# Layer 0 of a two-layer attention and mixture-of-experts kernel: other PSUM banks and other units for the small products

## The chip, the cores and the metric

The kernel runs on one core of a Trainium2 chip. The metric is the time of one execution on the device in microseconds. Each engine (TensorE, VectorE, ScalarE, GpSimd and the queue engine SyncE) runs its own list of instructions in order, and the engines hold each other by semaphores.

## What is computed

The input `x` has 64 batches of 64 channels by 256 positions, and `ctx_2048` has the same shape. Two layers follow each other, and each has an attention part and a mixture-of-experts part:

```python
x = x + _L0_xattn_ref(_layernorm(x), ctx_2048, ...)   # 8 heads of 8 channels, rotary, softmax over 256 positions
x = x + _L0_ffn_ref(_layernorm(x), ...)               # 64 experts, the best 8 of each row, silu(g) * u
x = x + _L1_xattn_ref(_layernorm(x), ctx_2048, ...)   # the same attention without rotary and output projection
x = x + _L1_ffn_ref(_layernorm(x), ...)               # 64 experts with a capacity
# _L0_xattn_ref, per batch:
q, k, v = heads(Wq x + bq), heads(Wk c + bk), heads(Wv c + bv)
q, k = rotary(q), rotary(k)
out = softmax(q k^T / sqrt(8)) v
return Wo out + bo
```

## The kernel before

The 64 batches are handled as 32 pairs; a pair fills the 128 partitions (2 batches of 64 channels). The attention stage of a layer is a software pipeline of 41 steps. A pair passes through it in stages that lie a fixed number of steps apart (`LAG`): load, comb, front (projection and rotation of q and k), stack (rearranging them by DMA), smax (row maxima of the scores), attn (exponentials and value products), back (division, output projection, residual), route (router logits), place and post (choice of slots, scatter). So one step works on up to eight pairs at once, each in another stage: pair s-2 is in front, s-4 in smax, s-5 in attn, s-6 in back, s-7 in route.

Each step has 16 units. In every unit TensorE makes one score product (`scores`, bank `psS`) for the pair in smax and the transposed score products (`scores_t`, two matmuls, bank `psE`) for the pair in attn; VectorE takes the maximum of the first (`red`), and ScalarE the exponential of the second (`prob`). Value products follow in groups of sixteen after units 7, 11, 15 and 2 of the next step. All else is placed by hand at fixed units: the instructions of an engine in a unit are issued in the order in which the `if` lines stand.

The small products share two PSUM banks, `psM[0]` and `psM[1]`. `MISC` lists them in the order in which TensorE makes them in a step, each with its stage; in the kernel before an item's bank is its place in the list modulo 2. `Step.before(item)` finds the item that used the same bank last, and `bank()` makes TensorE wait until that one has been read (`FREE`: for `OT0` and `OT1` the writing of `nrm`, for `V` the copy to `v`, for `K` and `Q` the rotation, for `NT` the write of `nt`, for `XT` the copy `xT`, for `mT0` the write of `mlo`). In layer 0 the banks are in this order: `mT1` 0, `RK` 1, `V` 0, `K` 1, `OT0` 0, `OT1` 1, `Q` 0, `NT` 1, `mT0` 0, `XT` 1, `WO` 0, `LG` 1.

The items that the change touches:

- `Q` (`q_rows`, line 1567, made by `product`, line 1564): two float32 products of the layer-normalised rows `xn`, for q and for q with its channels rolled. `xn` is made by ScalarE (line 963), which needs `rstd` from GpSimd (`roots`, lines 785 to 790). VectorE rotates the result (`rotate(0)`, lines 1157 and 1159), and GpSimd sums the halves (`rotated`, line 798).
- `OT0`, `OT1` (line 1562): the attention output `osb`, transposed, two transposes for each group of heads h. Each row holds 8 sums per head and the sum of exponentials. VectorE inverts that (`invert`, line 1139) and multiplies (`normalise`, line 1147) into `nrm`.
- `NT` (line 1562): `nrm` transposed back, two transposes; ScalarE writes it with its bias to `nt` (line 946), which `WO` (unit 12) multiplies by the output projection.
- `mT0` (line 1562): the maxima of the first half of the units, transposed; ScalarE makes their high part `mhi` (line 910), VectorE the low part `mlo` (line 1132), and SyncE sends both to the stacked `q` (line 686). The transposed scores of unit 0 of the next step wait for them.
- `XT` (line 1562, unit 10): `xr` transposed for the router; ScalarE copies it to `xT` (line 955).

Of the kernel before, what the change touches and what calls it, by code (L numbers as in the profile page):

```python
# [31 lines left out]
P = 128  # L32
B, C, T = 64, 64, 256
NH, HC = 8, 8
PAIRS = B // 2
TOKENS = B * C
E, I, K = 64, 96, 8
# [3 lines left out]
HALF = 16  # L41
# [68 lines left out]
def units_of_sum(s0):  # L110
    if s0 >= FULL:
        return ADDED, TWO, ONE, ALL, MOMENTS
    if s0 == FULL - 1:
# [9 lines left out]

MISC = {
    layer: [("mT1", "attn"), ("RK", "place"), ("V", "smax"), ("K", "front"), ("OT0", "back"), ("OT1", "back"),
            ("Q", "front"), ("NT", "back"), ("mT0", "smax"), ("XT", "route"), *last]
    for layer, last in enumerate(((("WO", "back"), ("LG", "route")), (("LG", "route"), ("LIST", "post"))))
}


class Step:
# [40 lines left out]
    def before(self, item):  # L172

        names = [name for name, _ in MISC[self.L]]
        i = names.index(item)
        bank, s = i % 2, self.s0
        while s >= 0:
            i -= 2
            if i < 0:
                i, s = i + len(names), s - 1  # L180
            if (self.L, s, names[i]) == (1, FULL - 2, "Q"):
                continue
            if 0 <= s - LAG[MISC[self.L][i][1]] < PAIRS and s >= 0:
                return bank, MISC[self.L][i], Step(self.L, s, self.it)
        return bank, None, None

# [11 lines left out]
def build(nc, x, ctx, tables, wts, out):  # L198
    stack = ExitStack()
    with stack:  # L200
# [231 lines left out]
        def lastbuf(st, stage, per=16):  # L432
# [3 lines left out]

        FREE = dict(mT0=s_mlo[0], mT1=s_mlo[1], V=s_v, OT0=s_nrm[0], OT1=s_nrm[1], Q=s_qr, K=s_kr,
                    NT=s_nt, WO=s_x1, XT=s_xT, LG=s_logit, RK=s_tot, LIST=s_list)
# [21 lines left out]

        def head_cols(tile, o, n):

            return tile[:, 0:2 * P].rearrange("p (h r) -> p h r", r=HALF)[:, :, o:o + n]

# [5 lines left out]
        def item_bank(L, name):  # L470
            return [n for n, _ in MISC[L]].index(name) % 2

# [414 lines left out]
        def _(act):  # L887
# [5 lines left out]
            def body(st):  # L893
# [19 lines left out]
                for u in range(UNITS):  # L913
# [27 lines left out]
                    if u == 3:  # L941
                        o_out("back", 1)
                    if L == 0 and u == 8 and st.on("back"):
                        act.wait_ge(s_ntp, st.n("back"))
                        wait(act, s_wo, last(st, "back"))
                        a.activation(nt[:, :], psM[item_bank(0, "NT")][:, 0:T], ACT.Identity,
                                     bias=bias[:, 7:8]).then_inc(s_nt, 1)
# [4 lines left out]
                    if u == (10, 11)[L] and st.on("route"):  # L952
                        act.wait_ge(s_xtp, st.n("route"))
                        wait(act, s_lgp, last(st, "route"))
                        a.copy(xT[:, :, :].rearrange("p c t -> p (c t)"), psM[item_bank(L, "XT")][:, 0:2 * P]).then_inc(s_xT, 1)
                    if u == 9 and st.on("smax"):
                        max_rows("smax", 0)
                    if u == (14 if filled else 6) and (st.on("front") or st.on("route")):
                        act.wait_ge(s_rstd, 4 * st.roots())
                    if u == (14 if filled else 6) and st.on("front"):  # L960
                        b = st.buf("front")
                        wait(act, s_qp, last(st, "front", back=NB))
                        a.activation(xn[b][:, :], (xin, x2)[L][b][:, :], ACT.Identity, bias=rstd[:, 1, 0:1],
                                     scale=rstd[:, 0, 0:1]).then_inc(s_xn, 1)
# [75 lines left out]
        def _(dve):  # L1040
# [77 lines left out]
            def body(st):  # L1118
# [16 lines left out]
                def invert(h):  # L1135

                    ps = psM[item_bank(L, f"OT{h}")]
                    dve.wait_ge(s_ot[h], st.n("back"))
                    ch.add(v_.reciprocal(rec[:, h, :], head_cols(ps, 8, 1).rearrange("p h o -> p (h o)")), f"rec{h}")

                def normalise(h):

                    ps = psM[item_bank(L, f"OT{h}")]
                    wait(dve, s_ntp, last(st, "back"))
                    ch.join(f"rec{h}")
                    r = rec[:, h, :]
                    v_.tensor_tensor(nrm[:, h, :].rearrange("p (h c) -> p h c", c=HC), head_cols(ps, 0, HC),  # L1147
                                     bass.AP(r.tensor, r.offset, [list(r.ap[0]), [1, UNITS], [0, HC]]),
                                     ALU.mult).then_inc(s_nrm[h], 1)

                def rotate(i):

                    b = st.buf("front")
                    ps = psM[item_bank(0, "QK"[i])]
                    dve.wait_ge((s_qp, s_kp)[i], st.n("front"))
                    wait(dve, s_qk, last(st, "front"))
                    v_.scalar_tensor_tensor(rope[:, 0, i, :], ps[:, 0:T], bias_c[:, 2 * i:2 * i + 1], cos[:, :],
                                            ALU.add, ALU.mult)
                    v_.scalar_tensor_tensor(rope[:, 1, i, :], ps[:, T:2 * T], bias_c[:, 2 * i + 1:2 * i + 2], sin[:, :],
                                            ALU.add, ALU.mult).then_inc((s_qr, s_kr)[i], 1)  # L1160
# [49 lines left out]
                for u in range(UNITS):  # L1210
# [21 lines left out]
                    if L == 1 and u == 8 and st.on("back"):  # L1232
# [5 lines left out]
                                                xres[b][:, :], ALU.add, ALU.add).then_inc(s_x1, 1)  # L1238
                    if u == 10 and st.on("smax") and not filled:
                        split_max("smax", 0)  # L1240
# [37 lines left out]
                    if L == 0 and u == 4 and st.on("front"):  # L1278
                        if st.s0 == LAG["front"]:
                            dve.wait_ge(d_table, 16 * 3 * HC)  # L1280
                        rotate(1)
                    if u == 5 and st.on("back"):
                        invert(0)
                    if u == 6 and st.on("back"):
                        normalise(0)
                        invert(1)
                    if u == 7 and st.on("back"):
                        normalise(1)
                    if L == 0 and u == 7 and st.on("front"):
                        rotate(0)  # L1290
                    if u == 0 and st.on("post") and L == 1:
# [213 lines left out]
        def _(pe):  # L1505
# [3 lines left out]
            def body(st):  # L1509
# [62 lines left out]
                for u in range(UNITS):  # L1572
# [11 lines left out]
                    if u == 2:  # L1584
                        values("back", 3)
                    if u == 7 and st.on("front") and not (L == 1 and st.s0 == FULL - 2):
                        q_rows(st)
# [6 lines left out]
                    if u == 3 and st.on("smax"):  # L1594
                        b = st.buf("smax")
                        product("V", "smax", [(d_ctx[b], st.nbuf("smax"))],
                                [(ctx_t[b][:, i * P:(i + 1) * P], wbd[L]["v"][:, :]) for i in range(2)], s_vp, P)
                    if u in (5, 6) and st.on("back"):
                        h = u - 5
                        product(f"OT{h}", "back", [(s_oev, st.n("back", 2))],  # L1600
                                [(osb[:, half, h * P:(h + 1) * P], None) for half in range(HALVES)], s_ot[h])
                    if u == 8 and st.on("back"):
                        product("NT", "back", [(s_nrm[0], st.n("back")), (s_nrm[1], st.n("back"))],
                                [(nrm[:, h, :], None) for h in range(2)], s_ntp)
                    if u == 9 and st.on("smax"):
                        product("mT0", "smax", [(s_max, st.n("smax", UNITS, 8))],
                                [(mx[st.buf("smax")][:, 0, :], None)], s_mT[0])
# [142 lines left out]
```

## Time and profile before

| | us |
|---|---|
| median of 3 runs | 2037.71 (2036.14 to 2038.18) |
| the profiled execution | 2035.62 |
| its span | 2033.8 |
| TensorE matmuls busy | 1634.2 (80%) |
| VectorE busy | 1412.9 (69%) |
| ScalarE busy | 1230.3 (60%) |
| GpSimd busy | 986.1 (48%) |

The shares are means over the attention stage of layer 0 (to about 600 us), its expert stage, the attention stage of layer 1 and its expert stage, which have different limits. For the change the reader needs the first stage alone, and in it one step of the pipeline.

### The profile page before, as it was taken

To read this page: it belongs to the slowest core of one execution; us is meant where nothing else is said; L and a number is where in the kernel's file an instruction comes from. 1 tells how busy PE (TensorE), PEld (TensorE's weight loads), DVE (VectorE), ACT (ScalarE), POOL (GpSimd) and SP (SyncE) were. 2 spreads that over 40 slices of the span, in tenths; PEclk is the share of its full clock that TensorE was granted. 3 is DMA by queue.
4 is the path that set the end of the run, shared out by engine and by line. 5 is a ranking of instruction groups with operands and counts; after the bars stand their busy time and mean duration, and the time that the engine had idled before them with its cause. 6 is when DMAs were issued, how large, how long until landed. Compare 5 with 4: busy or idle time off the path is not lost. (4 is left out here: it accounts for less than half of the span.)

```text
span 2033.8 us, 44372 instructions
## 1 busy us (share of the span) xinstructions
PE 1634.2 (80%) x12470; PEld 1095.2 (54%) x12623; DVE 1412.9 (69%) x4341; ACT 1230.3 (60%) x3174; POOL 986.1 (48%) x1114
## 2 busy tenths in 40 slices
PE   3999999999974999999997278888888888855551
PEld 1555555555543889888886134444444444444430
DVE  5888899999954445545434489999999999743330
ACT  1777777777752566666665268778878777621110
POOL 4367777777763000000001776666666662158883
PEclk9999999999986999999999589999999999979996
DMA  5688878777757976666665678887877775178856
GB/s 141 159 211 249 240 215 217 214 216 213 207 159 225 289 213 202 195 200 198 196 199 169 163 188 219 224 224 198 202 193 195 197 198 144 49 198 185 176 93 112
DMA packets 413085, 390.94 MB, mean 192 GB/s; under 512 B 46640, under 2 KB 385072, under 8 KB 412848
## 3 DMA queue, kind: packets, MB, share of 16 engines
q1 hardware_dynamic: 346496, 265.28, 49.2%
q0 software_dynamic: 37904, 90.22, 16.9%
q10 hardware_dynamic: 28448, 32.59, 5.5%
q8 instruction: 111, 1.82, 0.4%
q14 instruction: 126, 1.03, 0.2%
HBM read 233.74 MB, written 170.16 MB: 199 GB/s over the span
## 5 line engine op out<-in xcount | busy, mean ns | idle before, releaser
L1125 DVE TENSOR_REDUCE mx<-psS 128x2 f32<-128x512 f32 x1024 | 679.0, 674 | 86.5 <-PE psS L1518 59.0
L923 ACT ACTIVATE prob<-psE 128x512 f32<-128x512 f32 x1024 | 594.4, 591 | 235.8 <-PE psE L1531 219.2
L772 POOL DMA_INDIRECT yg<-y_d,row_all x256 | 248.4, 970 | 630.8 <-SPq L413 480.0
L1531 PE MATMUL psE<-q,k 128*128 128x256 bf16 x2048 | 394.1, 275 | 30.7 <-issue 10.2
L1518 PE MATMUL psS<-k,q 128*128 128x512 bf16 x871 | 336.5, 388 | 27.0 <-DVE mx L1125 14.1
L1470 DVE TENSOR_TENSOR hid<-sil,psE 128x96 f32<-128x96 f32 x384 | 97.7, 254 | 331.0 <-ACT sil L1024 331.0
L1643 PE MATMUL psE<-wt,xgT 128*128 (+1 forms) x1536 | 323.9, 335 | 2.1 <-ACT xgT L1019 1.6
L759 POOL DMA_INDIRECT xs_d<-xr,row_all x256 | 251.5, 982 | 94.4 <-ACT prob L923 46.1
L1531 PEld LDWEIGHTS psE<-q,k 128*128 128x128 bf16 x2048 | 187.1, 98 | 181.3 <-ACT prob L923 62.6
L1549 PE MATMUL psO<-prob,v 128*32 128x256 f32 x4096 | 275.0, 386 | 0.0
L1019 ACT COPY xgT<-psS 128x256 f32<-128x256 f32 x384 | 144.6, 376 | 186.7 <-PE psS L1637 160.7
L1643 PEld LDWEIGHTS psE<-wt,xgT 128*128 128x128 f32 x1536 | 246.6, 194 | 7.8 <-issue 5.9
L1637 PE MATMUL psS<-ident,xg 128*128 128x128 f32 x768 | 153.9, 282 | 104.7 <-DMA xg<-xn_d,idx 88.8
L1655 PE MATMUL psM<-wt,hT 96*128 (+1 forms) x768 | 231.5, 383 | 0.0
L1637 PEld LDWEIGHTS psS<-ident,xg 128*128 128x128 f32 x768 | 103.5, 143 | 165.4 <-DMA xg<-xn_d,idx 92.0
L1518 PEld LDWEIGHTS psS<-k,q 128*128 128x128 bf16 x1024 | 103.6, 101 | 146.8 <-issue 87.4
L1028 ACT COPY y_all<-psM 128x256 f32<-128x256 f32 x320 | 119.1, 372 | 87.9 <-PE psM L1655 87.6
L1549 PEld LDWEIGHTS psO<-prob,v 128*32 128x32 f32 x4096 | 107.1, 109 | 95.7 <-issue 47.7
L1024 ACT ACTIVATE sil<-psE 128x96 f32<-128x96 f32 x384 | 96.3, 251 | 93.1 <-PE psE L1643 92.4
L1655 PEld LDWEIGHTS psM<-wt,hT 96*128 96x128 f32 x768 | 117.0, 193 | 14.8 <-issue 0.4
L1564 PE MATMUL psM<-xn,proj_q 128*128 128x256 f32 x126 | 44.5, 436 | 86.8 <-DVE nrm L1147 50.4
L818 POOL TENSOR_TENSOR parts<-rem,parts 128x512 bf16<-128x512 f32 x64 | 74.7, 1168 | 44.2 <-ACT parts L997 42.6
(220 smaller groups left out, 2539.0 us busy)
## 6 DMA issues: line engine op xcount, KB each, us to landing
xg<-xs_d SPq DMA_DIRECT2D x320, 128.0 KB, 2.6
y_d<-y_all SPq DMA_DIRECT2D x320, 128.0 KB, 2.3
q<-q_stack_d SPq DMA_DIRECT2D x128, 256.0 KB
k<-k_stack_d SPq DMA_DIRECT2D x128, 256.0 KB
wt<-in_gu ACTq DMA_DIRECT2D x110, 192.0 KB, 2.9
q_stack_d<-parts SPq DMA_DIRECT2D x64, 192.0 KB
k_stack_d<-parts SPq DMA_DIRECT2D x64, 192.0 KB
wt<-in_dn ACTq DMA_DIRECT2D x110, 96.0 KB, 3.6
```

The costliest lines, as they stand in the source:

```text
L759: g.indirect_dma_start(xs_d[:, :], bass.IndirectOffsetOnAxis(row_all[:, row(st.pair(stage) * K + k, 1)], 0), xr[b][:, 0:T], None).then_inc ...
L772: g.indirect_dma_start(yg[:, k, :], None, y0_d[:, :], bass.IndirectOffsetOnAxis(row_all[:, row(st.pair("load") * K + k, 1)], 0))\
L923: a.activation(prob[gr][:, u % 4, :], psE[ring][:, :], ACT.Exp, scale=SCALE).then_inc(s_exp, 1)
L1019: a.copy(xgT[st.buf("X", 2)][:, :, :].rearrange("p c t -> p (c t)"), psS[st.buf("X", 2)][:, 0:2 * P]).then_inc(s_xgT, 1)
L1028: a.copy(y[st.buf("D")], psM[st.buf("D", 2)][:, 0:T]).then_inc(s_y, 1)
L1125: v_.tensor_reduce(mx[b][:, bg // 4, :].rearrange("p (h r) -> p h r", h=2)[:, :, (bg % 4) * 2 + tt], psS[(UNITS * (st.s0 - LAG["smax"]) + ...
L1518: m_.matmul(psS[(UNITS * (st.s0 - LAG["smax"]) + u) % 3][:, :], q2[b][:, bg, tt * P:(tt + 1) * P], k2[b][:, bg, :], start=True, stop=True) ...
L1531: ins = m_.matmul(psE[ring][:, i * T:(i + 1) * T], k2[b][:, bg, hh * T + i * P:hh * T + (i + 1) * P], q2[b][:, bg, :], start=True, stop=True)
L1549: ins = m_.matmul(psO[32 * j:32 * j + 32, half * T:(half + 1) * T], v[b][:, i, unit_at(4 * q + j), :], prob[gr][:, j, i * T:(i + 1) * T], ...
L1637: ins = m_.transpose(psS[i][:, c * P:(c + 1) * P], xg[b][:, c * P:(c + 1) * P], ident[:, :])
L1643: ins = m_.matmul(psE[i][:, 0:2 * I], xgT[i][:, c, :], weights_of(st, "GU", table, P, 2 * I * c, 2 * I), start=(c == 0), stop=(c == 1))
L1655: m_.matmul(psM[i][:, 0:T], hT[i][:, :], weights_of(st, "D", table, I, 4 * I, T), start=True, stop=True).then_inc(s_yp, 1)
```

## The change

In layer 0 alone `MISC` now names the bank of each item, and the order is another: `mT1` 0, `RK` 1, `V` 0, `K` 1, `Q` 0, `OT` 1, `NT` 0, `mT0` 1, `XT` 0, `WO` 0, `LG` 1. `OT0` and `OT1` become one item `OT` of four transposes, all in bank 1. The units become:

| | before | after |
|---|---|---|
| `xn` on ScalarE, with the wait for `rstd` | 6 | 4, ahead of the copy of `v` |
| `Q` on TensorE | 7 | 5 |
| rotation of q on VectorE | 7 | 6 |
| transposes of the output | 5 and 6 | 6 |
| `invert` and `normalise` | 5, 6, 7 | all at 7 |
| `NT` on TensorE, `nt` on ScalarE | 8 | 9 |
| `mT0`, `mhi` | 9 | 10 |
| `mlo` of the first half | 10 | 11 |

Layer 1 keeps its banks and units. The core of the diff:

```diff
-MISC = {
-    layer: [("mT1", "attn"), ("RK", "place"), ("V", "smax"), ("K", "front"), ("OT0", "back"), ("OT1", "back"),
-            ("Q", "front"), ("NT", "back"), ("mT0", "smax"), ("XT", "route"), *last]
-    for layer, last in enumerate(((("WO", "back"), ("LG", "route")), (("LG", "route"), ("LIST", "post"))))
-}
+MISC = (
+    (("mT1", "attn", 0), ("RK", "place", 1), ("V", "smax", 0), ("K", "front", 1), ("Q", "front", 0),
+     ("OT", "back", 1), ("NT", "back", 0), ("mT0", "smax", 1), ("XT", "route", 0), ("WO", "back", 0),
+     ("LG", "route", 1)),
+    (("mT1", "attn", 0), ("RK", "place", 1), ("V", "smax", 0), ("K", "front", 1), ("OT0", "back", 0),
+     ("OT1", "back", 1), ("Q", "front", 0), ("NT", "back", 1), ("mT0", "smax", 0), ("XT", "route", 1),
+     ("LG", "route", 0), ("LIST", "post", 1)),
+)
...
-                    if L == 0 and u == 8 and st.on("back"):
+                    if L == 0 and u == 9 and st.on("back"):
...
-                    if u == 9 and st.on("smax"):
+                    if u == (10, 9)[L] and st.on("smax"):
                         max_rows("smax", 0)
-                    if u == (14 if filled else 6) and (st.on("front") or st.on("route")):
+                    if u == (14 if filled else (4, 6)[L]) and (st.on("front") or st.on("route")):
                         act.wait_ge(s_rstd, 4 * st.roots())
-                    if u == (14 if filled else 6) and st.on("front"):
+                    if u == (14 if filled else (4, 6)[L]) and st.on("front"):
...
-                    if u == 10 and st.on("smax") and not filled:
+                    if u == (11, 10)[L] and st.on("smax") and not filled:
                         split_max("smax", 0)
...
-                    if u == 5 and st.on("back"):
+                    if L == 0 and u == 6 and st.on("front"):
+                        rotate(0)
+                    if u == (7, 5)[L] and st.on("back"):
                         invert(0)
-                    if u == 6 and st.on("back"):
+                    if u == (7, 6)[L] and st.on("back"):
+                        if L == 0:
+                            invert(1)
                         normalise(0)
-                        invert(1)
+                        if L == 1:
+                            invert(1)
                     if u == 7 and st.on("back"):
                         normalise(1)
-                    if L == 0 and u == 7 and st.on("front"):
-                        rotate(0)
...
-                    if u == 7 and st.on("front") and not (L == 1 and st.s0 == FULL - 2):
+                    if u == (5, 7)[L] and st.on("front") and not (L == 1 and st.s0 == FULL - 2):
                         q_rows(st)
...
-                    if u in (5, 6) and st.on("back"):
+                    if L == 0 and u == 6 and st.on("back"):
+                        pe.wait_ge(s_oev, st.n("back", 2))
+                        ps = bank(pe, st, "OT")
+                        for h in range(2):
+                            for half in range(HALVES):
+                                ins = m_.transpose(ps[:, (2 * h + half) * P:(2 * h + half + 1) * P],
+                                                   osb[:, half, h * P:(h + 1) * P], ident[:, :])
+                            ins.then_inc(s_ot[h], 1)
+                    if L == 1 and u in (5, 6) and st.on("back"):
...
-                    if u == 8 and st.on("back"):
+                    if u == (9, 8)[L] and st.on("back"):
                         product("NT", "back", [(s_nrm[0], st.n("back")), (s_nrm[1], st.n("back"))],
                                 [(nrm[:, h, :], None) for h in range(2)], s_ntp)
-                    if u == 9 and st.on("smax"):
+                    if u == (10, 9)[L] and st.on("smax"):
                         product("mT0", "smax", [(s_max, st.n("smax", UNITS, 8))],
```

In layer 0 `invert` of either half waits for both pairs of transposes (`s_ot[1]`), and the readers of the banks follow the new layout.

## Rows read from the trace of the kernel before

**Rows 1.** Busy time by stretch: one step of the pipeline.

```profile
core 0: us, PE busy (x) PEld busy (x) DVE busy (x) ACT busy (x) POOL busy (x), PEclk, DMA share, GB/s
...
299.83:317.00 17.17, 16.12 (x141) 9.58 (x142) 15.52 (x47) 12.62 (x29) 12.82 (x16) 1.00 0.72 208
```

**Rows 2.** Waits from 100 to 650 us: total, times, longest.

```profile
ACT prob L923 <- PE psE L1531: 118.7, 152, 2.2
...
PE psM L1564 <- DVE nrm L1147: 20.5, 26, 0.8
```

**Rows 3.** TensorE in order of time, units 4 to 7: start, length, instruction.

```profile
312.71 0.66 PE L1564 MATMUL psM<-ctx,proj_k 128*128 128x256 f32 x2
...
313.64 0.38 PE L1518 MATMUL psS<-k,q 128*128 128x512 bf16 x1
313.85 0.38 PE L1531 MATMUL psE<-q,k 128*128 128x256 bf16 x2
314.07 0.38 PE L1562 MATMUL psM<-ident,osb 128*128 128x128 f32 x2
...
314.86 0.41 PE L1562 MATMUL psM<-ident,osb 128*128 128x128 f32 x2
315.32 0.38 PE L1531 MATMUL psE<-q,k 128*128 128x256 bf16 x2
316.49 0.67 PE L1564 MATMUL psM<-xn,proj_q 128*128 128x256 f32 x2 [0.79 <-DVE nrm L1147]
...
317.52 0.85 PE L1549 MATMUL psO<-prob,v 128*32 128x256 f32 x12
```

**Rows 4.** TensorE in order of time, units 7 to 10 and the next unit 0.

```profile
300.35 1.07 PE L1549 MATMUL psO<-prob,v 128*32 128x256 f32 x16
301.36 0.39 PE L1518 MATMUL psS<-k,q 128*128 128x512 bf16 x1
...
301.80 0.38 PE L1562 MATMUL psM<-ident,nrm 128*128 128x128 f32 x2
...
303.11 0.41 PE L1562 MATMUL psM<-ident,xr 128*128 128x128 f32 x2
...
308.78 0.38 PE L1531 MATMUL psE<-q,k 128*128 128x256 bf16 x2 [0.16 <-issue]
```

**Rows 5.** ScalarE in order of time, units 8, 4, 5 and 6.

```profile
302.00 0.60 ACT L923 ACTIVATE prob<-psE 128x512 f32<-128x512 f32 x1 [2.19 <-PE psE L1531]
302.50 0.47 ACT L946 ACTIVATE nt<-psM,bias 128x256 f32<-128x256 f32 x1
...
312.91 0.60 ACT L923 ACTIVATE prob<-psE 128x512 f32<-128x512 f32 x1 [0.17 <-PE psE L1531]
313.41 0.37 ACT L981 COPY v<-psM 128x256 f32<-128x256 f32 x1
314.27 1.25 ACT L923 ACTIVATE prob<-psE 128x512 f32<-128x512 f32 x2 [0.50 <-PE psE L1531]
315.42 0.59 ACT L963 ACTIVATE xn<-xin,rstd 128x256 f32<-128x256 f32 x1
```

**Rows 6.** VectorE in order of time, units 4 to 6.

```profile
313.84 0.48 DVE L1157 SCALAR_TENSOR_TENSOR rope<-psM,bias_c,cos 128x256 f32<-128x256 f32 x1 [0.26 <-PE psM L1564]
...
314.63 0.68 DVE L1125 TENSOR_REDUCE mx<-psS 128x2 f32<-128x512 f32 x1
...
315.30 0.25 DVE L1139 RECIPROCAL rec<-psM 128x16 f32<-128x16 f32 x1
315.47 0.63 DVE L1125 TENSOR_REDUCE mx<-psS 128x2 f32<-128x512 f32 x1
...
316.07 0.27 DVE L1147 TENSOR_TENSOR nrm<-psM,rec 128x128 f32<-128x128 f32 x1
```

**Rows 7.** GpSimd in order of time: the last of the root operations.

```profile
311.58 0.19 POOL L790 TENSOR_TENSOR rstd<-below,rstd 128x2 f32<-128x2 f32 x1
```

**Rows 8.** SyncE's queue in order of time: the low part of the maxima.

```profile
304.40 0.56 SPq L686 DMA_DIRECT2D q<-mlo  x1
```

More of the change, by code:

```diff
@@ L172, in before @@
     def before(self, item):
-        names = [name for name, _ in MISC[self.L]]
-        i = names.index(item)
-        bank, s = i % 2, self.s0
+        at = [bank for name, _, bank in MISC[self.L] if name == item][0]
+        shared = [(name, stage) for name, stage, bank in MISC[self.L] if bank == at]
+        i, s = [name for name, _ in shared].index(item), self.s0
         while s >= 0:
-            i -= 2
+            i -= 1
             if i < 0:
-                i, s = i + len(names), s - 1
-            if (self.L, s, names[i]) == (1, FULL - 2, "Q"):
+                i, s = i + len(shared), s - 1
+            name, stage = shared[i]
+            if (self.L, s, name) == (1, FULL - 2, "Q"):
                 continue
-            if 0 <= s - LAG[MISC[self.L][i][1]] < PAIRS and s >= 0:
-                return bank, MISC[self.L][i], Step(self.L, s, self.it)
-        return bank, None, None
+            if s >= 0 and 0 <= s - LAG[stage] < PAIRS:
+                return at, (name, stage), Step(self.L, s, self.it)
+        return at, None, None
 def steps(layer, body):
@@ L434, in lastbuf @@
             return st.nbuf(stage, per) - per
-        FREE = dict(mT0=s_mlo[0], mT1=s_mlo[1], V=s_v, OT0=s_nrm[0], OT1=s_nrm[1], Q=s_qr, K=s_kr,
+        FREE = dict(mT0=s_mlo[0], mT1=s_mlo[1], V=s_v, OT=s_nrm[1], OT0=s_nrm[0], OT1=s_nrm[1], Q=s_qr, K=s_kr,
                     NT=s_nt, WO=s_x1, XT=s_xT, LG=s_logit, RK=s_tot, LIST=s_list)
@@ L459, in over_e, with head_cols @@
             return tile.unsqueeze(2).broadcast_to((P, K, n))
-        def head_cols(tile, o, n):
-            return tile[:, 0:2 * P].rearrange("p (h r) -> p h r", r=HALF)[:, :, o:o + n]
+        def head_cols(L, h, o, n):
+            tile = psM[item_bank(L, ("OT", f"OT{h}")[L])]
+            first = (h, 0)[L] * 2 * P
+            return tile[:, first:first + 2 * P].rearrange("p (h r) -> p h r", r=HALF)[:, :, o:o + n]
         def ones_of(b, o):
@@ L470, in item_bank @@
         def item_bank(L, name):
-            return [n for n, _ in MISC[L]].index(name) % 2
+            return [at for n, _, at in MISC[L] if n == name][0]
         FLAG = dict(idx=0, gather=4, X=8, GU=9, H=10, D=11)
@@ L1135, in invert @@
                 def invert(h):
-                    ps = psM[item_bank(L, f"OT{h}")]
-                    dve.wait_ge(s_ot[h], st.n("back"))
-                    ch.add(v_.reciprocal(rec[:, h, :], head_cols(ps, 8, 1).rearrange("p h o -> p (h o)")), f"rec{h}")
+                    dve.wait_ge(s_ot[1 if L == 0 else h], st.n("back"))
+                    ch.add(v_.reciprocal(rec[:, h, :], head_cols(L, h, 8, 1).rearrange("p h o -> p (h o)")), f"rec{h}")
                 def normalise(h):
-                    ps = psM[item_bank(L, f"OT{h}")]
                     wait(dve, s_ntp, last(st, "back"))
@@ L1146, in normalise @@
                     r = rec[:, h, :]
-                    v_.tensor_tensor(nrm[:, h, :].rearrange("p (h c) -> p h c", c=HC), head_cols(ps, 0, HC),
+                    v_.tensor_tensor(nrm[:, h, :].rearrange("p (h c) -> p h c", c=HC), head_cols(L, h, 0, HC),
                                      bass.AP(r.tensor, r.offset, [list(r.ap[0]), [1, UNITS], [0, HC]]),
```

## The prediction, made before the result was known

> **What bounds the kernel now.** I read four views, in this order. First the busy times by stretch [rows 1]: the attention stage of layer 0, to which the whole edit belongs, is a pipeline of 41 steps, and one full step lasts 17.17 us. Its row has TensorE busy for 16.12 us of that at granted clock 1.00, VectorE for 15.52, ScalarE for 12.62, GpSimd for 12.82. So TensorE is the first limit, VectorE is only 1.65 us per step behind it, and the other two have over 4 us to spare. Second the waits of this stage [rows 2]: ScalarE waits 118.7 us for TensorE's transposed scores, which again puts TensorE ahead. TensorE's own waits are few, and the largest is 20.5 us, 26 times 0.79 us, for the normalised rows. Third TensorE's step in order of time [rows 3, 4], with the same stretch of ScalarE and VectorE beside it [rows 5, 6]. The same starts come back 17.17 us later in most steps (some early ones, in which ScalarE also issues weight loads, take 17.63), so I may put 301.36 and 318.53 for the same event.
>
> In rows 3 the reader is to see one hole. The pair of score products of unit 7 ends its slot at 315.54 (315.32 plus 0.22), and the query product behind it begins at 316.49: 0.95 us, of which the profile prints 0.79, as it counts the modelled tail of the matmul as busy. The cause is a bank: the query product writes bank 0, where the item before it is the first transposed result, and that is free only when VectorE has written `nrm` at 316.07, 0.27 long [rows 6]. From 316.34 to 316.49 gives 0.15 us as the time that a release takes to TensorE. The activation of `xn` at 315.42, 0.59 long [rows 5], would have let it go at about 316.16.
>
> **The change part by part.** It happens in the 28 steps in which both a front and a back pair are on (28 of the 41; elsewhere one of the two is missing). Matmul and vector work are the same in amount. What moves is order and three waits. I work the step through again from unit 4, with slots taken from starts: a pair of score products 0.43 (313.64 to 314.07), two transposes 0.22, a projection product of two 0.93 to 1.03 (312.71 to 313.64, 316.49 to 317.52), a group of sixteen value products 1.01 (300.35 to 301.36) [rows 3, 4].
>
> *ScalarE, unit 4.* `xn` now stands between the exponential and the copy of `v`. The exponential begins at 312.91 and gives way after 0.50; `xn` 313.41, the copy at 313.91, its 0.37 us end at 314.28. The exponential of unit 5 can't begin before its scores (314.27 now), so it loses nothing. The moved wait for `rstd` has the `v` copy and all later exponentials behind it; GpSimd's last root operation ends at 311.77 [rows 7], 1.6 us before, so I cost it at nothing; without that cover each late microsecond would be a microsecond of the step.
>
> *TensorE, unit 5.* The query product stands behind the pair that ends at 314.07. It waits for `xn` (314.00) and for bank 0, whose former item is now the value product, so for the copy of `v`: 314.28 plus 0.15 is 314.43. The hole shrinks from 0.95 to 0.36. From both sides: 0.08 if only `xn` held it, 0.6 if the copy came 0.25 later. I take 0.36, because each of its three durations has a row.
>
> *Unit 6 and 7.* The product takes 0.93 to 1.03, I take 0.95: 315.38. Pair to 315.81, four transposes to 316.24, pair to 316.67, value products from 316.75 (the same 0.08 as before) to 317.76. The four transposes need the key product's bank, free since the rotation ended near 314.71. The same bank now makes the second pair of transposes begin at 314.86 and not at 314.72, so 0.14 us goes with it.
>
> *VectorE.* The reduction of unit 6 begins 0.42 after its scores (313.85 to 314.27 is what ScalarE shows for that delay) at 315.80, 0.60 later the rotation of q, 0.79 for its two instructions (313.84 to 314.63), to 317.19; the reduction of unit 7 to 317.79; then two reciprocals at 0.17 (315.30 to 315.47) and two multiplications at about 0.19: the last begins near 318.32 and ends near 318.6. The queue behind these is the reductions of units 8 and 9; they start 0.4 us earlier than in the old step (318.5 against 318.95), so TensorE, which needs them three units later, doesn't wait.
>
> *Unit 9 and 10.* TensorE: pair of unit 8 to 318.20, of unit 9 to 318.64, transposes back at 318.75, held 0.1 by `nrm`. Then the pair of unit 10 and the transposed maxima, and it is at the transposes of `xr` at about 319.5. These use the bank of the transposes back, so they wait for ScalarE's `nt`. ScalarE: exponential of unit 8 at 318.40, of unit 9 at 318.90, `nt` at 319.40, 0.47 long, to 319.87 [rows 5]; plus 0.15 is 320.02. **This is the new hole, 0.5 us.** In the old step there was one unit more between the two, `nt` ended at 302.97 and the transposes of `xr` began at 303.11, hardly held: 0.11. The bounds of the new hole are 0, if something else lets `nt` go earlier, and 0.6.
>
> *Sum.* In the old step the transposes of `xr` begin at 303.11 + 17.17 = 320.28; now at 320.02. Gain 0.26 us a step: 0.59 at the query product and 0.14 at the second transposes, less 0.1 at `nrm`, 0.39 at `nt`, and rounding. What follows in the step is unchanged and moves with it. 28 times 0.26 is 7.3 us. In the four filling and the draining steps one hole shrinks (query product) and the other opens, together 0 within 2 us. Nothing after the stage depends on where in the steps the work stood, and the last steps are paced by exponentials that come earlier as well.
>
> The median is 2037.71 and the profiled execution took 2035.62 with a span of 2033.8, so I expect 2030.4 as a median and about 2026.5 as the span.
>
> *A rule against it.* TensorE's row 314.86 shows two result banks in use in turn, and the change puts four transposes in one. The Trainium skill (Perfetto Trace Analysis, Optimizing Tensor Performance) says that independent groups should rotate through banks, so that the evacuation of one runs beside the next. By that rule the divisions, which now start only after all four transposes, ought to come late and hold TensorE. That they end near 318.6, just where TensorE asks for them, is the row-by-row answer above; what it would cost if the rule wins is rival C.
>
> **The rivals.**
>
> A, *the full hole closes and no new one opens*: `nt` doesn't hold the transposes of `xr`. Then the gain is 0.26 + 0.5, and 28 times 0.76 is 21.3 us: 2016.4. For it: ScalarE is idle 2.19 us just before the exponential of unit 8 [rows 5], so it has room. Against it: the two exponentials and `nt` in a row have 1.47 us of their own from 318.40 on, and TensorE has less than that before it.
>
> B, *the gain is given back at the step's start*. The low part of the first half's maxima moves from unit 10 to 11: VectorE ends it at about 321.7, and the queue issues its transfer at about 321.75 instead of 321.57 (304.40 + 17.17) [rows 8], while the first transposed scores that need it stand 0.26 earlier than 308.78. Now there are 4.38 us between issue and use, then 3.94. No wait for it appears before, so landing takes less than 4.38 as a rule; if it takes more than 3.94 it costs up to 0.44 us a step, 12 us in all, and cancels the gain. With half of that, 2036. The small transfer argues for early landing; the DMA share of 0.72 in this step [rows 1] against.
>
> C, *slower: the divisions bind*. The transposes back may come at 319.0 without moving `nt`, which ScalarE can't begin before 319.40. If VectorE, with only 1.65 us of free time in a step and now with the rotation and a reduction ahead of four small instructions, ends the second multiplication later than about 318.85, every further tenth is on the path. No row shows two reciprocals and two multiplications in a run. If they took their full lengths (0.25 and 0.27 [rows 6]) and were held 0.15 each by the semaphore between them, the end would be near 319.2 and `nt` 0.37 later; with the reduction of unit 8 (0.6) on top, 0.97 later. Less the gain of 0.26 that is 0.11 to 0.71 us a step, 3 to 20 us: 2041 to 2058. It turns to a loss once the second multiplication ends after 319.1.
>
> D, *nothing at all*: the step is held by a loop through another engine. GpSimd has 4.35 us free and DMA landings aren't in the waits, so this is weak; 2037.7.
>
> **How the numbers follow.** Forecast 0.58, A 0.13, B 0.14, D 0.06, C 0.09. The forecast's own range is 0.1 to 0.45 us a step with 2 us for the ends: 2023 to 2036. The range for 8 in 10 reaches most of the way to A and past B: 2019 to 2038.5. What the measurement can tell from no change is about 0.2%, 4.1 us. Faster by more than this: the forecast but for its weak end, and A: 0.68. Within it: that end, B and D: 0.23. Slower: C: 0.09.
>
> **What the profile after would show.** The step (start of a query product to the next) at 16.9 us in place of 17.17. The query product right behind the pair of unit 5, held 0.3 to 0.4 by the copy of `v`; the wait of the query product for `nrm` gone from layer 0. Four transposes in one run. A repeated hole before the transposes of `xr`, released by `nt`. GpSimd's sum of the rotated halves about a microsecond earlier. A step of 16.4 us with no hole at `xr` is A; waits of the transposed scores of unit 0 for a transfer of `mlo` are B; the transposes back held by `nrm` for over half a microsecond are C. The forecast is wrong from the start if `xn` comes later than I have it, for instance held by `rstd`.

## The result

The changed kernel takes 2028.24 us (median of 6 runs, 2026.57 to 2028.78) against 2037.95 for the kernel before in the same comparison (6 runs, 2036.14 to 2044.08): ratio 0.9946, 95% interval 0.9933 to 0.9959. Its profiled execution took 2026.57 us with a span of 2024.9; before it was 2035.62 and 2033.8. The forecast was 2030.4 with a span of 2026.5.

The page of the kernel after, its first part (busy time, share of the span, instructions):

```profile
PE 1633.4 (81%) x12470; PEld 1095.1 (54%) x12623; DVE 1412.4 (70%) x4341; ACT 1236.0 (61%) x3174; POOL 989.1 (49%) x1114
```

Most of the gain, 7.5 of the 8.9 us of span, lies in the attention stage of layer 0. The product of the normalised rows with the output weights (`nt` with `proj_o`) comes once in a step, so its first and last starts show how long the 31 step intervals took (below, a step is the time between two such starts). Its group (count, shortest/median/longest ns, first and last start), first before, then after:

```profile
L1564 PE MATMUL psM<-nt,proj_o x64: 378/382/526, 79.9 to 597.2; 128*128 128x256 f32 x64
```

```profile
L1571 PE MATMUL psM<-nt,proj_o x64: 379/380/454, 77.8 to 589.7; 128*128 128x256 f32 x64
```

The first comes 2.1 us earlier and the last 7.5 us earlier, so 5.4 us were won between the two. The median step went from 17.17 to 16.85 us. One step of after, by stretch, to be held against [rows 1] (same columns):

```profile
301.11:317.96 16.85, 16.22 (x148) 9.60 (x142) 15.56 (x46) 12.81 (x30) 12.85 (x16) 1.00 0.80 217
```

TensorE is busy for as long as before (16.22 us, 16.12 before) and the step is shorter by idle time alone. TensorE from unit 5 to the transposes of `xr`, after (start, length, instruction, idle before and its releaser), against [rows 3, 4]:

```profile
310.09 0.38 PE L1525 MATMUL psS<-k,q 128*128 128x512 bf16 x1
310.31 0.38 PE L1538 MATMUL psE<-q,k 128*128 128x256 bf16 x2
310.83 0.67 PE L1571 MATMUL psM<-xn,proj_q 128*128 128x256 f32 x2
...
312.21 0.60 PE L1610 MATMUL psM<-ident,osb 128*128 128x128 f32 x4
...
313.17 1.07 PE L1556 MATMUL psO<-prob,v 128*32 128x256 f32 x16
...
315.18 0.41 PE L1569 MATMUL psM<-ident,nrm 128*128 128x128 f32 x2
...
315.87 0.27 PE L1569 MATMUL psM<-ident,mx 128*16 128x128 f32 x1
316.41 0.41 PE L1569 MATMUL psM<-ident,xr 128*128 128x128 f32 x2 [0.28 <-ACT nt L952]
```

The query product begins 0.30 us after the pair of unit 5 ends its slot (310.31 plus 0.22 to 310.83); before, the hole was 0.95. The four transposes run in one group with no wait. The new hole stands where it was forecast, before the transposes of `xr`, and is 0.43 us (the slot of the maxima is 0.11, as 315.39 to 315.50 in `e4_nt8` below, so 315.98 to 316.41; 0.28 by the profile's count of the modelled tail). ScalarE and VectorE beside it, against [rows 5, 6]:

```profile
309.84 0.59 ACT L969 ACTIVATE xn<-xin,rstd 128x256 f32<-128x256 f32 x1
310.33 0.36 ACT L987 COPY v<-psM 128x256 f32<-128x256 f32 x1
...
314.82 1.09 ACT L929 ACTIVATE prob<-psE 128x512 f32<-128x512 f32 x2 [0.84 <-PE psE L1538]
315.79 0.48 ACT L952 ACTIVATE nt<-psM,bias 128x256 f32<-128x256 f32 x1
```

```profile
313.64 0.68 DVE L1131 TENSOR_REDUCE mx<-psS 128x2 f32<-128x512 f32 x1
314.24 0.36 DVE L1144 RECIPROCAL rec<-psM 128x16 f32<-128x16 f32 x2
314.59 0.49 DVE L1151 TENSOR_TENSOR nrm<-psM,rec 128x128 f32<-128x128 f32 x2
```

The copy of `v` ends at 310.69 and the query product starts 0.14 later; `nt` ends at 316.27 and the transposes start 0.14 later. These are the two releases of the forecast. The divisions end at 315.08, and the transposes back start 0.10 after that.

Waits of the whole stage, 60 to 600 us, after (total us, times, longest), to be held against [rows 2], which are of 100 to 650 us:

```profile
PE psM L1569 <- ACT nt L952: 9.7, 31, 0.7
...
PE psE L1538 <- DMA q<-mlo: 3.5, 3, 1.8
...
PE psS L1525 <- DMA k<-k_stack_d: 1.1, 1, 1.1
```

The wait of the query product for `nrm`, 26 times 0.8 us before, is no longer there. The waits of TensorE's matmuls for transfers are new: the kernel before has none in this stretch.

### The profile page after: what moved, and what is told of

It is laid out like the page before. It is cut to its first block and busy times, and to the rows that moved or that the text cites. A ratio compares the mean times of both kernels' runs of the same rounds, so it can differ in the third digit from the quotient of the medians.

```text
span 2024.9 us, 44338 instructions
## 1 busy us (share of the span) xinstructions
PE 1633.4 (81%) x12470; PEld 1095.1 (54%) x12623; DVE 1412.4 (70%) x4341; ACT 1236.0 (61%) x3174; POOL 989.1 (49%) x1114
```

## The experiments

Two theories were open. *The forecast's own*: the time is the sum of the holes of the step, so closing a hole is worth its length. *The rival*: something else paces the step (ScalarE's row of exponentials, the divisions, a late transfer), so a hole that is closed opens elsewhere. The first four kernels ran on one chip, where the kernel before took 2036.89 us (median of 11 runs).

**Transposes of `xr` one unit later** (`e1_xt11`), which gives `nt` more time:

```diff
-                    if u == (10, 11)[L] and st.on("route"):
+                    if u == 11 and st.on("route"):
                         act.wait_ge(s_xtp, st.n("route"))
...
-                    if u == 10 and st.on("route"):
+                    if u == (11, 10)[L] and st.on("route"):
                         b = st.buf("route")
```

> The changed kernel with the transposes of xr (and their copy) one unit later, at 11. Theory (the wait for nt holds TensorE in every step): the hole before the transposes of xr, 0.43 us in the changed kernel, is gone, the step goes from 16.85 to about 16.5 us, and the whole is 8 to 12 us faster than the changed kernel: about 2018. Rival (the step is held by a loop elsewhere, the hole is only where the slack lies): the hole moves, for instance to the projection WO, which now waits sooner for xT, the step stays at 16.8 to 16.9 and the time at 2028.

Measured: 2025.36 us, ratio 0.9942 (0.9919 to 0.9966), median step 16.80. TensorE, then ScalarE:

```profile
316.53 0.44 PE L1569 MATMUL psM<-ident,xr 128*128 128x128 f32 x2
317.02 0.38 PE L1538 MATMUL psE<-q,k 128*128 128x256 bf16 x2
317.52 0.67 PE L1571 MATMUL psM<-nt,proj_o 128*128 128x256 f32 x2
```

```profile
317.01 0.37 ACT L961 COPY xT<-psM 128x256 f32<-128x256 f32 x1 [0.62 <-PE psM L1569]
```

The hole before the transposes of `xr` is gone. The kernel has the step of the rival and not the 16.5 us of the theory: a hole of 0.28 us stands before the output product (317.02 plus 0.22 to 317.52), whose bank is that of `xr` and comes free only with the copy to `xT`, ending at 317.38. The step gained 0.05 of the 0.43. So `nt` was not the only thing on the path: the same bank is handed on three times in close order, and moving one of them moves the hole.

**Transposes back and `nt` at unit 8 again** (`e4_nt8`):

```diff
-                    if L == 0 and u == 9 and st.on("back"):
+                    if L == 0 and u == 8 and st.on("back"):
                         act.wait_ge(s_ntp, st.n("back"))
...
-                    if u == (9, 8)[L] and st.on("back"):
+                    if u == 8 and st.on("back"):
```

> The changed kernel with the transposes back and nt at unit 8 in place of 9. Theory: nrm ends 0.56 us after TensorE reaches this place, so a hole of about 0.6 us opens there, and as nt is then 0.2 us earlier the hole before the transposes of xr closes: the step stays at 16.85 to 17.0 and the time at 2028 to 2032. Rival (divisions aren't late, the move to 9 was needless): the step falls to 16.5 and the time to 2018.

Measured: 2025.7 us, ratio 0.9947 (0.9929 to 0.9966), median step 16.81. TensorE:

```profile
314.27 0.41 PE L1569 MATMUL psM<-ident,nrm 128*128 128x128 f32 x2 [0.40 <-DVE nrm L1151]
...
315.39 0.27 PE L1569 MATMUL psM<-ident,mx 128*16 128x128 f32 x1
315.50 0.38 PE L1569 MATMUL psM<-ident,xr 128*128 128x128 f32 x2
```

One hole was traded for another, as expected: the transposes back now stand 0.56 us behind the pair of unit 8 (313.71 to 314.27; the profile counts 0.40) and wait for `nrm`, and those of `xr` follow the maxima without a gap. In the changed kernel the two holes are 0.12 and 0.43, 0.55 together. The chain (the divisions, the transposes back, `nt`, the transposes of `xr`) is as long as before, and where in it TensorE stands idle changes the step by 0.04 us.

**The maxima one unit earlier** (`e2_mt9`), so that the transfer of their low part has a unit more to land:

```diff
-                    if u == (10, 9)[L] and st.on("smax"):
+                    if u == 9 and st.on("smax"):
                         max_rows("smax", 0)
...
-                    if u == (11, 10)[L] and st.on("smax") and not filled:
+                    if u == 10 and st.on("smax") and not filled:
                         split_max("smax", 0)
...
-                    if u == (10, 9)[L] and st.on("smax"):
+                    if u == 9 and st.on("smax"):
                         product("mT0", "smax", [(s_max, st.n("smax", UNITS, 8))],
```

> The changed kernel with the transposed maxima of the first half, mhi and mlo back at units 9, 9 and 10. Theory (the later transfer of mlo costs TensorE a few one-off waits of 1 to 2 us at unit 0, but nothing in the steady step): the step stays at 16.85, the waits of the transposed scores for mlo go away, 1.5 to 3 us faster than the changed kernel: about 2026. Rival (these waits are chance collisions of transfers that the unit doesn't decide): same number of waits of over 1 us, 2028.

Measured: 2027.53 us, ratio 0.9955 (0.9937 to 0.9972), median step 16.85 as in after. Neither expectation came true: no wait for the low part is over 1 us, but three are still in the trace, of 0.28, 0.33 and 0.94 us, where after has 1.55, 1.83 and 0.16. The last output product starts at 587.57 and not 589.41. The total of this kernel is no different from the changed one's within the interval, so the time shows nothing. In an even step of this kernel the transfer is issued, and its reader starts, at:

```profile
298.82 0.56 SPq L692 DMA_DIRECT2D q<-mlo  x1
303.37 0.38 PE L1538 MATMUL psE<-q,k 128*128 128x256 bf16 x2 [0.16 <-issue]
```

That is 4.55 us, more than the 4.38 of the kernel before, which has no such wait in either of its two traces, and three waits remain. With the transfer at unit 11 there are 3.5 us of these waits in the trace of the changed kernel, 1.2 in `e1_xt11`, 0.9 in `e3_q7` and 2.1 in `e4_nt8`. So the 1.6 us of this kernel lie within what varies from trace to trace, and that the slack between issue and use decides the waits isn't shown. All of over 0.5 us, those for keys included, fall in two places of the stage, 132 to 152 us and 218 to 238 us; what is special there wasn't looked into.

**The new banks, with the query product left at unit 7** (`e3_q7`):

```diff
-                    if u == (14 if filled else (4, 6)[L]) and st.on("front"):
+                    if u == (14 if filled else 6) and st.on("front"):
...
-                    if u == (5, 7)[L] and st.on("front") and not (L == 1 and st.s0 == FULL - 2):
+                    if u == 7 and st.on("front") and not (L == 1 and st.s0 == FULL - 2):
```

(`rotate(0)` goes back behind the divisions of unit 7, and the wait for `rstd` to unit 6, with it.)

> The changed kernel's banks, with xn, the query product and its rotation back at units 6, 7 and 7. It tells the bank from the unit. If the bank alone closes the hole (the product no longer waits for nrm): the product follows the pair of unit 7 with only what xn holds it, 0.3 to 0.6 us, the step is 16.9 to 17.1, and the time 2029 to 2034. If the unit does it (xn comes too late for unit 7 and the rotation crowds the divisions, and the bank is only what makes the move possible): the step is 17.1 or more and the time 2034 to 2040.

Measured: 2032.3 us, ratio 0.9979 (0.9967 to 0.999), median step 17.09. Step and time lie at the upper edge of what was expected if the bank closes the hole. All that is left of the change here (the banks, the four transposes in one group, the divisions, transposes back and maxima at their later units) gives 0.08 us a step, and the earlier place of the query product, with `xn` and the rotation, the other 0.24 of the 0.32. The hole before the query product is 0.13 us here (314.64 plus 0.22 to 314.99), so it is closed too. Two others are what keeps the step long. The four transposes now wait for the rotation of the key product, and those of `xr` for `nt`:

```profile
313.96 0.63 PE L1610 MATMUL psM<-ident,osb 128*128 128x128 f32 x4 [0.19 <-DVE rope L1163]
314.64 0.38 PE L1538 MATMUL psE<-q,k 128*128 128x256 bf16 x2
314.99 0.70 PE L1571 MATMUL psM<-xn,proj_q 128*128 128x256 f32 x2
...
319.29 0.41 PE L1569 MATMUL psM<-ident,xr 128*128 128x128 f32 x2 [0.43 <-ACT nt L952]
```

The following kernels ran on a second chip, where the kernel before took 2134.88 us (median of 16 runs), 4.8% more than on the first. Only comparisons within one chip are used. Four went there together: the two kernels of the case once more (`a_again` the changed one, `b_again` the one before), and two others.

**The four transposes over two banks in turn** (`e5_two_banks`). This takes rival C's rule at its word:

```diff
-     ("OT", "back", 1), ("NT", "back", 0), ("mT0", "smax", 1), ("XT", "route", 0), ("WO", "back", 0),
+     ("OT0", "back", 1), ("OT1", "back", 0), ("NT", "back", 0), ("mT0", "smax", 1), ("XT", "route", 0), ("WO", "back", 0),
...
-                        ps = bank(pe, st, "OT")
                         for h in range(2):
+                            ps = bank(pe, st, f"OT{h}")
                             for half in range(HALVES):
```

(The columns that the transposes write and the divisions read follow.)

> The changed kernel with the second pair of output transposes in bank 0, behind the query product, so that the two groups rotate through both banks again, all units as in the changed kernel. Theory (one bank for all four is what makes the early query product possible): the second pair waits for the rotation of q on VectorE, 1.3 to 1.5 us, the step is 18.0 to 18.4 us, slower than the kernel before by 1 percent or more: 2055 to 2070. Rival (banks in rotation overlap the divisions with the transposes, and TensorE loses little): the step is 16.6 to 16.9 and the time 2023 to 2030.

Measured: 2147.55 us, ratio 1.0057 (1.0031 to 1.0083), slower than the kernel before, by 0.6% and not by the 1% or more that was expected, while the changed kernel is at 0.9869 on the same chip. Its undisturbed steps take 18.26 us, as expected. The waits of the stage (100 to 650 us) and the place:

```profile
PE psM L1610 <- DVE rope L1163: 41.3, 26, 2.3
```

```profile
301.98 0.44 PE L1610 MATMUL psM<-ident,osb 128*128 128x128 f32 x2 [2.12 <-DVE rope L1163]
```

The second pair of transposes stands right behind the query product and would use the same bank, so TensorE waits, 1.6 us on average, until VectorE has rotated that product. With two banks for all small products, one bank for the four transposes is what makes the early place of the query product possible.

**Transposes back in the other bank, and the rotation behind the divisions** (`n1_nt_bank`), meant to close both holes at once:

```diff
-     ("OT", "back", 1), ("NT", "back", 0), ("mT0", "smax", 1), ("XT", "route", 0), ("WO", "back", 0),
+     ("OT", "back", 1), ("NT", "back", 1), ("mT0", "smax", 0), ("XT", "route", 1), ("WO", "back", 0),
```

(with the units of `e4_nt8` and `e2_mt9`, and `rotate(0)` after the divisions of unit 7.)

> The changed kernel with the transposes back in bank 1 (behind the transposes of the output, whose reading they wait for anyway), maxima in bank 0, transposes of xr in bank 1; rotation of q behind the divisions in unit 7; transposes back and nt at unit 8; maxima at 9, 9 and 10. Theory (both holes that are left, at the transposes back and at those of xr, come from the rotation standing ahead of the divisions, so that nrm is late): nrm ends 0.8 us sooner, neither hole opens, only the one at the query product is left, the step falls from 16.85 to 16.3 to 16.5 and the time to 2012 to 2018. Rival (VectorE, busy 15.5 us of the step, or GpSimd takes over as the bound): the step stays over 16.7 us with waits for the maxima, 2023 to 2028.

> The changed kernel once more, unaltered. It tells what of its trace is of this execution and what returns: the steady step should be 16.85 again. If the waits for the low part of the maxima and for the stacked k (three of 1.1 to 1.8 us in the steps between 130 and 240 us) belong to the order of the transfers, they come back at the same steps with about the same sum, 4.5 us; if they are chance, their places and sum differ. Time 2027 to 2030.

> The kernel before once more, unaltered: step 17.17 again, no wait over 0.3 us of TensorE for the low part of the maxima; and whether the filling steps up to the first output projection take 79.9 us again or vary by the 2 us by which the changed kernel was ahead there.

Measured: `n1_nt_bank` 2109.1 us, ratio 0.9885 (0.9855 to 0.9916), median step 17.79. The changed kernel 2105.14, ratio 0.9869 (0.9832 to 0.9907), median step 17.67. The kernel before, in a single execution, 2132.48, median step 18.19. None of the times and steps that were expected came, as the steps on this chip are uneven. In `a_again` no matmul of the stage waits for a transfer: the three waits of the first trace don't return here, so the order of the transfers alone doesn't make them. The first output product of `b_again` starts at 79.8, where the kernel before had 79.9. The first step of the stage, the one that nothing has disturbed yet, is 16.02 us in `n1_nt_bank` and 16.48 in the changed kernel, so the edit does take 0.46 us out of it; the later steps on this chip give that back and more. The changed kernel's gain is 1.3% here where it is 0.5% on the first chip. The trace of `b_again` shows waits that go with it, first TensorE, then ScalarE:

```profile
291.14 0.38 PE L1531 MATMUL psE<-q,k 128*128 128x256 bf16 x2
293.45 0.70 PE L1564 MATMUL psM<-xn,proj_q 128*128 128x256 f32 x2 [1.93 <-ACT xn L963]
...
294.51 1.75 PE L1549 MATMUL psO<-prob,v 128*32 128x256 f32 x16
```

```profile
290.09 0.60 ACT L923 ACTIVATE prob<-psE 128x512 f32<-128x512 f32 x1 [0.44 <-issue]
292.31 0.60 ACT L923 ACTIVATE prob<-psE 128x512 f32<-128x512 f32 x1 [1.62 <-PE psE L1531]
292.81 0.59 ACT L963 ACTIVATE xn<-xin,rstd 128x256 f32<-128x256 f32 x1
```

ScalarE reaches `xn` late, behind an exponential that itself began late (1.98 us after its scores at 290.33, where 0.42 is usual; why isn't known), and the query product waits for it: in all 27.3 us in 18 waits from 100 to 650 us. After the longest of them the clock falls too. The stretches before and behind it (columns as in [rows 1]):

```profile
286.70:293.40 6.70, 4.48 (x30) 2.90 (x27) 5.31 (x18) 3.40 (x8) 3.58 (x5) 1.00 0.82 207
293.40:297.40 4.00, 3.95 (x25) 2.10 (x26) 2.16 (x5) 1.11 (x3) 2.21 (x2) 0.67 1.04 259
```

Sixteen value products, 1.07 us elsewhere, then take 1.75: the granted clock is 0.67 on average over these 4 us, that is the lower of its two levels (1.2 GHz) for two thirds of them, after 1.93 us of idle time. Before the hole it was 1.00. The changed kernel issues `xn` at unit 4, and in `a_again` no matmul waits for it; weight loads do 12 times, up to 0.5 us. From the first output product to the last, `a_again` takes 24.2 us less than `b_again` (538.1 and 562.3), against 5.4 on the first chip. That these waits make the difference is likely by their size, but no kernel that has them and differs in nothing else was run.

**The same on a third chip**, where the kernel before took 2122.56 us (median of 16 runs): `n1_nt_bank` once more as `n1_third`, the changed kernel as `a_third`, and `n2_rot6`, which is `n1_nt_bank` with one difference:

```diff
+                    if L == 0 and u == 6 and st.on("front"):
+                        rotate(0)
                     if u == (7, 5)[L] and st.on("back"):
...
-                    if L == 0 and u == 7 and st.on("front"):
-                        rotate(0)
```

> The same kernel as n1_nt_bank (transposes back in bank 1, rotation of q behind the divisions, transposes back at 8, maxima at 9 and 10), once more beside the changed kernel. On a chip where the changed kernel's step is an even 16.85 us: theory 16.3 to 16.5 us a step and 10 to 16 us less than the changed kernel; rival (VectorE or GpSimd is the bound below 16.8) a step of 16.7 or more and less than 4 us of gain.

> As n1_nt_bank, but with the rotation of q at unit 6, ahead of the divisions, as in the changed kernel. It tells the order of VectorE from the banks. Theory (the 0.8 us of the rotation ahead of the divisions is what makes nrm late): a hole of 0.4 to 0.6 us at the transposes back returns and the step is 16.75 to 16.85, 10 us slower than n1. Rival (the bank of the transposes back matters, not the order): the step is that of n1.

> The changed kernel a third time: step 16.85 and 2027 to 2030 us on a chip where the kernel before takes 2035 to 2038. If the three one-off waits of the first trace (for the low part of the maxima and the stacked k between 130 and 240 us, 4.5 us together) are tied to the order of transfers, they return at the same steps; the second trace, on a chip whose steps were uneven throughout, had none over 0.3 us.

Measured: `n1_third` 2103.81 us, ratio 0.9926 (0.9899 to 0.9952); `n2_rot6` 2108.07, ratio 0.994 (0.9918 to 0.9962); `a_third` 2098.96, ratio 0.9903 (0.9873 to 0.9934). The median steps are 17.84, 17.81 and 17.66, so the steps again weren't even, and none of the steps and totals that were expected came. `a_third` has one wait for the low part in the stage, of 0.48 us, at another place than the first trace. The intervals overlap in part, and on neither chip did the variant beat the changed kernel. The first step tells the order of VectorE from the banks: it is 16.02 us in `n1_third`, 16.43 in `n2_rot6` and 16.48 in `a_third`. So of the 0.46 us the place of the rotation gives 0.41, and the banks and units the other 0.05. In `n2_rot6` the hole that was expected is there, and in `n1_third` it is not:

```profile
92.29 0.41 PE L1569 MATMUL psM<-ident,nrm 128*128 128x128 f32 x2 [0.38 <-DVE nrm L1151]
```

 The variant's gain of half a microsecond in an undisturbed step may show on a chip whose steps are even, as on the first; it wasn't tried there, and that stays open.

## Why the prediction was right, point by point

- *What bounds the kernel.* Right: TensorE is busy for 16.22 us of a step of 16.85, and the gain is idle time of TensorE. One reading was off: the 1.65 us by which VectorE is said to be behind TensorE are its idle time in the step (17.17 less 15.52); behind TensorE's 16.12 it is only 0.60.
- *The query product.* The copy of `v` holds it, as forecast; `xn` begins at 309.84 and ends before it (310.43). The hole is 0.30 and not 0.36.
- *The four transposes.* One group, no wait, as forecast.
- *The divisions.* Counted from the value products of unit 7 the forecast had the last one end 1.85 us on (316.75 to 318.6); it ends 1.91 us on (313.17 to 315.08), and the transposes back are held 0.12, for a forecast 0.1. Two reciprocals take 0.36 us in a run and two multiplications 0.49, for 0.34 and 0.38 in the forecast.
- *The hole at `xr`.* Right in place and releaser, 0.43 and not 0.50. Together with the query product that makes a gain of 0.32 a step and not 0.26, some 1.7 us too little in 28 steps.
- *The ends of the stage.* "Together 0 within 2 us" holds, but only as a sum: the first output product is 2.1 us early, and the four last, draining steps lose 0.8. Of the 2.1 us 1.4 are the edit's: from the fourth key product (54.74 before, 54.01 after) to the first output product it is 25.2 us in both traces of the kernel before and 23.8 in all three of the changed one. The rest arose earlier, between the third and the fourth key product, where the traces of the kernel before have 14.1 and 14.2 us and those of the changed one anything from 13.0 to 14.3.
- *Rival B.* Given 0.14, it came true in part, and in another form. No step pays 0.2 to 0.4 us for a late low part; three steps have waits of 1.1 to 1.8 us and are 1.0, 1.0 and 1.5 us longer than their neighbours, 3.5 us together. Two of these waits (1.55 and 1.83 us) are for the low part, the third (1.13) for a load of keys, which the change didn't touch by its text. In the last of the three the transfer is issued, and its reader starts, at:

```profile
232.34 0.56 SPq L692 DMA_DIRECT2D q<-mlo  x1
```

```profile
237.95 0.39 PE L1538 MATMUL psE<-q,k 128*128 128x256 bf16 x2 [1.83 <-DMA q<-mlo]
```

  That is 5.6 us between them. The forecast inferred from the absence of a wait that landing takes less than 4.38 us as a rule. The slack did shrink to 3.94 (301.30 to 305.24), and most steps have no wait; but as `e2_mt9` has waits with a slack of 4.55, that the shrinking made these waits isn't shown.
- *The sum.* Step by step, before against after: 27 steps at 0.32 give 8.6 us. Six early steps, in which ScalarE issues weight loads, were 0.46 over the median before and are some 0.3 over it after, which gives 1.0. The three late transfers take 3.5 and the four last, draining steps 0.8. Small differences in two steps give 0.2. That is 5.5 us, against 5.4 read from the output products; with the 2.1 at the beginning it is 7.5. Another 0.7 us is won between the last output product and the first work of the expert stage (639.25 before, 631.02 after), and 0.7 behind that, to 8.9 of span. Why these two came isn't explained; the forecast had nothing change behind the stage.
- *Rival A* (no new hole) is refuted by the trace of after; `e1_xt11` shows in addition that its 0.5 us wasn't to be had by moving `xr`.
- *Rival C.* The divisions are not late. The Trainium skill (Perfetto Trace Analysis, Optimizing Tensor Performance) advises rotating independent groups through banks. Here the trace speaks against it: rotating the pairs makes the kernel slower than before (1.0057), since the other bank of the two was taken by the query product.
- *GpSimd's sum a microsecond earlier.* Wrong. The rotation of q does end earlier, but `qk` is held by the row scatter that stands ahead of it, which had itself waited for an exponential:

```profile
313.78 0.96 POOL L765 DMA_INDIRECT xs_d<-xr,row_all  x1 [1.85 <-ACT prob L929]
314.77 1.28 POOL L804 TENSOR_TENSOR qk<-rope 128x512 f32<-128x512 f32 x1
```

  Counted from the key product, `qk` starts 5.62 us on (309.15 to 314.77) where it was 5.89 before (312.71 to 318.60). Nothing on the path hung on it.

- *The range.* With 0.1 us a step and 2 us lost at the ends the forecast's slow end is 2036.9, not 2036; nothing hangs on it.

So the mechanism was right, and sizes were off: the steady term by 0.06 us a step, 1.3 us in 27 steps against 7.3; the six early steps, 1.0 us that the forecast hadn't; the ends of the stage, 1.3 us; what lies behind the stage, 1.4 us put at nothing; and the late transfers, which stood only with a rival, 3.5 us the other way. That the sum came out within 2 us (7.3 forecast, 8.9 measured in the span) owes something to their cancelling.

## What to carry to other kernels

When several small results share two banks, read the order of handover, not the number of banks: each item is late by whoever evacuates the one before it, so the cheap gain is to put an item behind one that is evacuated early. Once the largest hole of such a chain is closed, moving the next item mostly moves the hole (0.43 us became 0.28 in another place, or 0.12 and 0.43 became 0.56, each for some 0.05 us of step). That one trace has no wait for a transfer doesn't show how much margin it has: the waits came in all five traces with even steps of the changed kernel and its variants, from 0.9 to 4.5 us together, and with a slack of 4.55 us as well as of 3.94.

## What the runs showed of the hardware

The three chips differ by more than the change is worth: the kernel before takes 2037 us on the first, 2135 and 2123 on the others, while the profiled execution of the changed kernel has about the same granted clock on each (0.950, 0.944 and 0.947 over the span). There the steps are uneven (17.2 to 20.7 us in `b_again`), and ScalarE shows more idle time that the profile puts down to nothing but issue. Before the exponentials it is 8.5 us in `before`, 26.7 in `b_again` and 22.9 in `a_third`, from 100 to 600 us, as in this row of `a_third`:

```profile
314.54 0.60 ACT L929 ACTIVATE prob<-psE 128x512 f32<-128x512 f32 x1 [0.55 <-issue]
```

What delays the instructions there wasn't found. The lengths of the instructions themselves are the same (the exponential 0.60 us on each chip). The same change was worth 1.0 and 1.3% on those chips and 0.5% on the even one.
